# A third residual buffer, a fifth transposed context and new turn tables for a four-layer transformer kernel

## The chip, the cores and the metric

One Trainium2 chip, one of its cores. The metric is the device time of one run of the kernel in microseconds (us); smaller is better. A core has five engines that run side by side, each through its own instruction list: PE (matmul), DVE (vector), ACT (activation functions and copies), POOL (elementwise work) and SP (which here only issues DMAs). They meet through semaphores.

## What is computed

The reference runs eight batches of 256 rows by 256 columns through four layers of attention and feed-forward work, each with a residual addition. Cut to its frame:

```python
x = x + L0_xattn(layernorm(x), ctx)              # 16 heads of 16, softmax
x = x + L0_ffn(layernorm(x), gate_w, expert_w)   # one expert of eight for each row
x = x + L1_xattn(layernorm(x), ctx)              # 16 heads, with a fixed mask
x = x + L1_ffn(layernorm(x), ...)                # three cycles: small nets give a factor, x += factor * twist(x)
x = x + L2_xattn(layernorm(x), ctx)              # linear attention
x = x + L2_ffn(layernorm(x), ...)                # linear layer and two of eight low-rank experts
x = x + L3_xattn(layernorm(x), ctx, mask)        # one head
x = x + L3_ffn(layernorm(x), ...)                # silu(x wg) * (x wu), then wd
```

Every batch goes through all four layers by itself; batches share only the weights.

## The kernel before

The kernel is written straight for the five engines. Each engine's program is a set of threads (Python generators) that emit instructions: `p` prepares an attention (norm, projections, splitting the projections into bf16 parts), `s` is the scores with their softmax, `v` the products with the values, the output projection and the experts of layer 0, `a` the net of layer 1's feed-forward part and linear attention, `b` the rest of layers 2 and 3 for batches 0 to 6, and `c` the same for batch 7. On PE there are two more, `w` and `z`, early and late fillers: every step of theirs issues two matmuls of a constant bf16 tile `blank` into a bank that nobody reads (`spin`, L2002 to L2004). They compute nothing.

What order the instructions of an engine stand in is decided by one string for each engine in `TURNS`: `weave` (L169) reads it letter by letter and lets the named thread go one step. An engine then works strictly through that list, and an instruction whose semaphore is not there yet holds up all that stands behind it. Moving a letter therefore changes no work, only who waits behind whom. Threads `w` and `z` run only as often as their letters occur: 106 and 54 times, which with the 16 filler matmuls ahead of all threads makes 336.

The attentions of layers 0 and 1 run in the order (batch 0, layer 0), (1, 0), (0, 1), (2, 0), (1, 1), and so on, so that two or three batches are under way at any time. The parts of this machine that the change and the prediction touch:

- The scores of a head are computed twice. `L1629` gives them for the row maximum, which DVE reduces (`L1177`). The maximum goes back into the operands by a small transpose (`L1695`) and a copy by ACT (`L873`). `L1714` then gives the transposed scores, ACT takes their exponential into `PT` (`L886`), and `L1736` multiplies with the values. The transposed scores have one PSUM bank, so that the next pair of `L1714` waits for ACT's `L886` on the pair before.
- `L1657` is the product with the eight experts of layer 0 (32 wide matmuls for a batch), which DVE adds up by `L1230`.
- `L1318` on DVE is the step x + factor * twist(x) of layer 1's net: two pairs of quarter tiles, cc with one sign and cn with the other.
- `L634`, `L635` and `L637` on POOL split the keys of an attention into bf16 parts (`kparts`). POOL also computes the scale of every norm (`L615` to `L630`).
- `XB` holds the residual rows of a batch from the end of layer 1's attention until they are stored. There are two, and the first write for batch b waits on DVE until the store of batch b - 2 has landed (semaphore `stored`, L1293 and L1294).
- `ctxT` holds transposed contexts, `CTX` of them: three buffers and the place of the weight wq3t, which is free again by the time a fourth context comes.

## Time and profile before

| what | value |
|---|---|
| median of three runs | 987.79 us (986.56 to 989.19) |
| span of the profiled execution | 986.1 us |
| PE busy | 949.3 us (96%) |
| of that in filler matmuls (`blank`) | 44.7 us, 336 of them |
| DVE, ACT, POOL busy | 634.1, 536.3, 221.5 us |

Busy time is the time in which an engine has an instruction under way, and the matmuls of PE overlap each other a little. The fillers count as busy, so PE's share says less than it seems at the two ends of the program, where most fillers are. The program has three stages for this purpose: a start, in which weights arrive and the first batches fill the machine, a long middle from about 228 to 892 us without any filler, and an end in which batch 7 runs alone.

### The profile page before, as it was taken

The numbers are of one execution on the slowest core, as the hardware profiler recorded it, in microseconds if no ns is written. First come the engines' busy times: TensorE is split into PE (matmuls) and PEld (weight loads), VectorE is DVE, ScalarE is ACT, GpSimd is POOL, SyncE is SP. The second block draws the span as 40 slices with busy tenths as digits, with TensorE's granted clock in tenths as the row PEclk, the third lists the DMA queues.
The fourth block names the chain that finished last, engine by engine and source line by source line (L and its number), as shares of the span: only waits on it lengthen the run. The fifth ranks groups of instructions, "written<-read, shape, count | busy, mean of one in ns | idle before, by whom it ended". The sixth has DMA issues, their size and how long they took to land.

```text
span 986.1 us, 17493 instructions
## 1 busy us (share of the span) xinstructions
PE 949.3 (96%) x6126; PEld 702.7 (71%) x6126; DVE 634.1 (64%) x2245; ACT 536.3 (54%) x1097; POOL 221.5 (22%) x317
## 2 busy tenths in 40 slices
PE   8999999989999999999999999999999999999998
PEld 6665665757687766778687766776686757777777
DVE  4634674675675776867586776775776676736564
ACT  1341644776368643875448644866376544864421
POOL 3104311303240132403141023302321032012210
PEclk9999999999999999999999999999999999999999
DMA  7308535400540023520432104402132004000000
GB/s 261 58 30 226 127 113 113 88 10 17 113 94 9 11 50 70 113 49 13 80 73 46 44 1 86 98 11 49 27 67 59 12 17 92 1 12 1 1 1 22
DMA packets 41078, 58.27 MB, mean 59 GB/s; under 512 B 4096, under 2 KB 35840, under 8 KB 37376
## 3 DMA queue, kind: packets, MB, share of 16 engines
q1 hardware_dynamic: 39600, 48.59, 23.6%
q10 hardware_dynamic: 1392, 8.56, 2.3%
q8 instruction: 50, 0.82, 0.3%
q14 instruction: 36, 0.29, 0.1%
HBM read 41.67 MB, written 13.89 MB: 56 GB/s over the span
## 4 chain that ended last, share of the span: by engine, by line
PE 77%; ACT 9%; DVE 8%; issue 4%; POOL 1%; DMA 1%; ACTq 0%; SPq 0%; DVEq 0%; POOLq 0%
PE bank L1657 11%; PE bank L1984 6%; PE bank L1517 6%; PE bank L1736 6%; PE bank L1714 6%; PE bank L1508 6%; PE bank L1629 4%; PE bank L1995 4%; PE bank L1771 4%; PE bank L1765 3%; PE bank L1717 3%; ACT PT L886 2%; ACT QA L873 2%; PE bank L1797 2%; PE bank L1526 2%
## 5 line engine op out<-in xcount | busy, mean ns | idle before, releaser
L886 ACT ACTIVATE PT<-bank 128x512 f32<-128x512 f32 x256 | 153.0, 598 | 127.4 <-PE bank L1717 71.8
L1657 PE MATMUL bank<-w,xhT 128*128 128x512 f32 x256 | 126.8, 599 | 0.0
L1714 PE MATMUL bank<-QA,KA 104*128 104x256 bf16 x512 | 112.7, 273 | 12.4 <-ACT PT L886 10.5
L1184 DVE CUSTOM_DVE_ANT_0 bank<-bank,maskb 128x256 f32<-128x256 f32 x256 | 101.7, 450 | 25.7 <-PE bank L1629 25.4
L1177 DVE TENSOR_REDUCE mx<-bank 128x2 f32<-128x512 f32 x128 | 83.6, 684 | 28.9 <-PE bank L1629 28.5
L1629 PE MATMUL bank<-KA,QA 96*128 96x256 bf16 x512 | 91.1, 273 | 1.9 <-DVE mx L1184 0.8
L1984 PE MATMUL bank<-xhBT,wi 128*128 128x256 f32 x336 | 87.0, 390 | 2.9 <-DVE hT L1491 2.5
L1714 PEld LDWEIGHTS bank<-QA,KA 104*128 104x128 bf16 x512 | 46.5, 99 | 60.3 <-issue 45.8
L1230 DVE SCALAR_TENSOR_TENSOR x<-bank,one,x 128x256 f32<-128x256 f32 x128 | 61.5, 481 | 21.6 <-PE bank L1657 17.6
L873 ACT COPY QA<-bank 8x256 bf16<-8x256 bf16 (+1 forms) x128 | 67.8, 575 | 10.1 <-PE bank L1695 8.8
L1984 PEld LDWEIGHTS bank<-xhBT,wi 128*128 128x128 f32 x336 | 59.2, 191 | 12.9 <-DVE hT L1491 5.6
L1629 PEld LDWEIGHTS bank<-KA,QA 96*128 96x128 bf16 x512 | 47.5, 100 | 25.3 <-DVE mx L1184 3.2
L1717 PE MATMUL bank<-maskb,identb 128*128 128x256 bf16 x256 | 63.5, 273 | 0.0
L1736 PE MATMUL bank<-PT,vaug 128*32 128x256 f32 x1024 | 63.2, 388 | 0.0
L615 POOL TENSOR_TENSOR veps_s<-mv_s,epsm 128x2 f32<-128x2 f32 x16 | 3.1, 194 | 255.3 <-DVE mv_s L1067 255.3
L1657 PEld LDWEIGHTS bank<-w,xhT 128*128 128x128 f32 x256 | 42.0, 190 | 20.8 <-issue 17.1
L1771 PE MATMUL bank<-xhAT,w 128*128 128x256 f32 (+1 forms) x216 | 49.5, 361 | 0.3
L629 POOL TENSOR_TENSOR veps_a<-mv_a,epsm 128x2 f32<-128x2 f32 (+1 forms) x18 | 3.6, 198 | 204.7 <-DVE mv_a L1067 202.3
L1736 PEld LDWEIGHTS bank<-PT,vaug 128*32 128x32 f32 x1024 | 30.4, 111 | 25.9 <-issue 9.9
L2004 PE MATMUL bank<-blank 128*128 128x256 bf16 x336 | 44.7, 279 | 1.1 <-POOL blank L743 1.1
L1279 DVE RECIPROCAL rc<-bank 128x8 f32<-128x8 f32 x64 | 13.0, 203 | 49.1 <-PE bank L1749 48.4
L1995 PE MATMUL bank<-wi,hT 128*128 128x256 f32 x168 | 42.2, 382 | 0.1
(311 smaller groups left out, 2028.3 us busy)
## 6 DMA issues: line engine op xcount, KB each, us to landing
QA<-scratch SPq DMA_DIRECT2D x90, 128.0 KB, 4.8
scratch<-kparts SPq DMA_DIRECT2D x30, 192.0 KB, 2.4
KA<-scratch SPq DMA_DIRECT2D x15, 384.0 KB, 4.6
scratch<-qparts SPq DMA_DIRECT2D x30, 192.0 KB, 2.3
KA<-scratch SPq DMA_DIRECT2D x15, 256.0 KB, 5.5
w<-pack ACTq DMA_DIRECT2D x1, 2345.0 KB, 8.3
wi<-ipack ACTq DMA_DIRECT2D x1, 2304.0 KB, 8.5
xin<-x_in SPq DMA_DIRECT2D x8, 256.0 KB, 6.3
```

Source lines behind the costliest of these rows:

```text
L873: act.copy(QA[m][KR:KM, g * GH + lo:g * GH + hi, :], ot_b16[KR:KM, 512:512 + S].unsqueeze(1).to_broadcast([MR, hi - lo, S])).then_inc(negm ...
L886: act.activation(PT[:, n % RING, :, :].rearrange("p t s -> p (t s)"), st_bank[:, :], ACT.Exp).then_inc(exp_s, 1)
L1177: dve.tensor_reduce(mx[:, i % 4, n % GH, :], s_bank[n % 2][:, :].rearrange("p (t s) -> p t s", t=T), AX.X, ALU.max).then_inc(max_s, 1)
L1184: last = dve.tensor_tensor_reduce(s, s, maskb[:, t, :], op0=ALU.add, op1=ALU.max, scale=1.0, scalar=-HUGE, accum_out=mx[:, i % 4, n % GH, ...
L1629: last = pe.matmul(s_bank[n % 2][:, t * S:(t + 1) * S], QA[m][0:KR, u, t * P:(t + 1) * P], KA[m][0:KR, u, :], start=True, stop=True)
L1657: last = pe.matmul(bank[n % 2][:, :], xhT[:, kk, t * P:(t + 1) * P], W("exp0", KT)[:, kk, i * 512:(i + 1) * 512], start=(kk == 0), stop=(k ...
L1714: last = pe.matmul(st_bank[:, t * S:(t + 1) * S], KA[m][0:KM, v, t * P:(t + 1) * P], QA[m][0:KM, v, :], start=True, stop=(m == 0))
L1717: last = pe.matmul(st_bank[:, t * S:(t + 1) * S], identb[:, :], maskb[:, t, :], start=False, stop=True)
L1736: last = pe.matmul(pv_bank[32 * h:32 * h + 32, g % 2 * S:(g % 2 + 1) * S], vflat[m][:, t, (g * GH + h) * VW:(g * GH + h) * VW + 32], PT[:, ...
L1771: last = pe.matmul(ps[:, k * S + lo * P:k * S + hi * P], W(name, KT)[:, kk, k * P:(k + 1) * P], src[:, kk, lo * P:hi * P], start=(kk == 0) ...
L1984: last = pe.matmul(ps[:, i * S + lo * P:i * S + hi * P], ww[:, kk, k * P:(k + 1) * P], L.xhBT[:, kk, lo * P:hi * P], start=(kk == 0), stop ...
L1995: last = pe.matmul(ps[:, t * D:(t + 1) * D], hid[:, kk, t * P:(t + 1) * P], wd[:, kk, :], start=(kk == 0), stop=(kk == HT - 1))
```

## The change

`XB` gets a third buffer and `ctxT` a fifth, and every string in `TURNS` is replaced. In the core of the diff the lines that only replace `b % 2` by `b % NX` are left out, and of the strings the beginning of one stands for all:

```diff
-CTX = 4
+CTX = 5
+NX = 3
...
     "tensor":
-        "pppwwwppwwwwwwwwwwwwwwwwppwwwwwwwwwwwwpwwwwwpwpwwwwwwppwwwwwwwwwwwwwwwwwwwsswwspspssvsvswwvsvpsvswwv"
+        "wpppwpwwwwwpwwpwwwpwwpwwwwpwwwpwwwpwwwwpwwwwswswwswpswspvsvwswsvswwspvwvwwwsswvvspvvswsvpwwwvwswvvwv"
...
-        XB = [sb(f"XB{i}", [P, T, D]) for i in range(2)]
+        XB = [sb(f"XB{i}", [P, T, D]) for i in range(NX)]
...
-                        if b >= 2:
-                            dve.wait_ge(stored, nth(stored, b - 2, 16))
-                        update(XB[b % 2], ot_bank, xb1, added)
+                        if b >= NX:
+                            dve.wait_ge(stored, nth(stored, b - NX, 16))
+                        update(XB[b % NX], ot_bank, xb1, added)
```

Each thread has as many letters as before, but for PE's fillers: `w` goes from 106 to 77 and `z` from 54 to 33, so that 236 filler matmuls are left of 336. By `CTX` the tile that the last batch takes for its gate (`sg`, `p3T`) is now `ctxT[3]`, before `ctxT[0]`. The line numbers after the change are one higher from L40 on.

What the strings do is seen in the instruction lists. PE in the first part of the start: `L1508` and `L1517` are projections of batch 0. `L1517` here gives the values, which DVE adds a bias to and writes into `vaug` (semaphore `v_s0`), and `L1535`, the first step of preparing linear attention, waits for that. Before:

```order
L1508 MATMUL bank<-xh0T,w 128x256 x3
L2004 MATMUL bank<-blank 128x256 x32
L1517 MATMUL bank<-w,ctxT 128x256 [waits k_f0,w_in2]
L1517 MATMUL bank<-w,ctxT 128x256 x3
L2004 MATMUL bank<-blank 128x256 x24
L1535 MATMUL bank<-w,ctxT 128x16 [waits q_f0,v_s0]
```

and now:

```order
L1518 MATMUL bank<-w,ctxT 128x256 [waits k_f0,w_in2]
L1518 MATMUL bank<-w,ctxT 128x256
L2005 MATMUL bank<-blank 128x256 x6
L1518 MATMUL bank<-w,ctxT 128x256 x2
L2005 MATMUL bank<-blank 128x256 x4
L1536 MATMUL bank<-w,ctxT 128x16 [waits q_f0,v_s0]
```

The 24 fillers ahead of the wait for `v_s0` have become four.

PE just ahead of the first scores of the program, which wait for `q_first` and `k_first` (the first queries and keys have landed); `L1560` is the last step of preparing linear attention's operands (`sx`). Before:

```order
L1556 MATMUL bank<-w,xh0T 128x16 [waits third_dve]
L1560 MATMUL bank<-w,sx 128x256 [waits third_dve]
L1560 MATMUL bank<-w,sx 128x256
L2004 MATMUL bank<-blank 128x256 x38
L1629 MATMUL bank<-KA,QA 128x256 [waits q_first,k_first]
```

and now:

```order
L1557 MATMUL bank<-w,xh0T 128x16 [waits third_dve]
L2005 MATMUL bank<-blank 128x256 x8
L1561 MATMUL bank<-w,sx 128x256 [waits third_dve]
L1561 MATMUL bank<-w,sx 128x256
L2005 MATMUL bank<-blank 128x256 x8
L1630 MATMUL bank<-KA,QA 128x256 [waits q_first,k_first]
```

The 38 fillers that stood last before the first scores have become eight, and eight more stand one step ahead.

DVE in batch 5's net, at about 738 us: the four steps of `L1318`, among maxima of scores (`mx`, `mq`) and the last multiplications of the gate (`sg`, `hT`) that PE waits for. Before:

```order
L1177 TENSOR_REDUCE mx<-bank 128x2 [waits s_ps]
L1196 TENSOR_SCALAR mq<-mx 128x2x4 [waits mT_ps,max_s]
L1197 SCALAR_TENSOR_TENSOR mq<-mx,mq 128x2x4 [waits dve_s]
L1318 SCALAR_TENSOR_TENSOR o<-xhA,cc 128x2x64
L1318 SCALAR_TENSOR_TENSOR o<-xhA,cn 128x128
L1318 SCALAR_TENSOR_TENSOR o<-xhA,cc 128x2x64
L1318 SCALAR_TENSOR_TENSOR o<-xhA,cn 128x128
L1489 SCALAR_TENSOR_TENSOR sg<-sg,bank 128x256 [waits sg_s]
L1491 TENSOR_TENSOR hT<-sg,bank 128x256 [waits dve_b]
```

and now:

```order
L1490 SCALAR_TENSOR_TENSOR sg<-sg,bank 128x256 [waits sg_s]
L1492 TENSOR_TENSOR hT<-sg,bank 128x256 [waits dve_b]
L1178 TENSOR_REDUCE mx<-bank 128x2 [waits s_ps] x2
L1319 SCALAR_TENSOR_TENSOR o<-xhA,cc 128x2x64
L1319 SCALAR_TENSOR_TENSOR o<-xhA,cn 128x128
L1178 TENSOR_REDUCE mx<-bank 128x2 [waits s_ps]
L1197 TENSOR_SCALAR mq<-mx 128x2x4 [waits mT_ps,max_s]
L1198 SCALAR_TENSOR_TENSOR mq<-mx,mq 128x2x4 [waits dve_s]
L1490 SCALAR_TENSOR_TENSOR sg<-sg,bank 128x256 [waits sg_s]
L1492 TENSOR_TENSOR hT<-sg,bank 128x256 [waits dve_b]
```

One gate multiplication now stands ahead of the net's step, and the step is in two pairs: the second comes after two more gate multiplications.

## Rows read from the trace of the kernel before

**Rows 1.** The page: the span, and busy time of each engine

```profile
span 986.1 us, 17493 instructions
...
PE 949.3 (96%) x6126; PEld 702.7 (71%) x6126; DVE 634.1 (64%) x2245; ACT 536.3 (54%) x1097; POOL 221.5 (22%) x317
```

**Rows 2.** Stretches: length, busy of PE, PEld, DVE, ACT, POOL; granted clock, DMA share, GB/s

```profile
0.00:70.00 70.00, 61.29 (x451) 45.84 (x452) 30.91 (x82) 24.57 (x52) 12.33 (x25) 1.00 0.41 113
70.00:228.00 158.00, 147.13 (x937) 97.84 (x936) 99.25 (x349) 85.16 (x176) 38.59 (x46) 0.98 0.46 110
228.00:730.00 502.00, 497.32 (x3194) 370.36 (x3193) 346.04 (x1219) 297.10 (x591) 130.79 (x178) 1.00 0.26 53
730.00:750.00 20.00, 17.98 (x123) 12.95 (x122) 16.56 (x35) 12.83 (x26) 4.71 (x5) 0.91 0.53 117
...
892.00:986.10 94.10, 86.60 (x546) 71.92 (x543) 52.40 (x211) 30.59 (x96) 14.51 (x32) 0.98 0.02 6
```

**Rows 3.** Stretches of the tile blank alone: length, busy of PE, PEld, ACT, POOL

```profile
0.00:70.00 70.00, 24.77 (x186) 18.75 (x186) 0.20 (x1) 0.31 (x1) 1.00 0.41 113
...
892.00:986.10 94.10, 13.90 (x108) 10.48 (x107) 0.00 (x0) 0.00 (x0) 0.98 0.02 6
```

**Rows 4.** Tile XB: a store (start, duration); its first writes (duration, first and last start)

```profile
879.74 0.39 SPq L589 DMA_DIRECT2D out<-XB  x1
...
L1253 DVE TENSOR_TENSOR XB<-bank,xb x8: 657/690/692, 174.7 to 892.3; 128x512 f32<-128x512 f32 x8
```

**Rows 5.** PE's timeline in the start: start, duration, instruction [idle before, releaser]

```profile
18.79 2.78 PE L2004 MATMUL bank<-blank 128*128 128x256 bf16 x24
22.48 1.06 PE L1535 MATMUL bank<-w,ctxT 128*128 128x16 f32 x8 [0.91 <-DVE vaug L1089]
```

**Rows 6.** Ahead of the first scores: chain of waits; SP's timeline; page on DMA issues

```profile
31.33 4.15 PE bank L2004 x38
...
25.93 3.25 SPq L528 DMA_DIRECT2D QA<-QA  x3
...
QA<-scratch SPq DMA_DIRECT2D x90, 128.0 KB, 4.8
```

**Rows 7.** 93 to 100 us: stretch, timelines of PE, DVE, POOL; undisturbed L1080 (ns)

```profile
96.00:98.00 2.00, 2.00 (x7) 1.53 (x6) 0.00 (x0) 0.64 (x5) 1.14 (x1) 0.50 0.94 114
...
94.95 0.66 PE L1526 MATMUL bank<-w,xh 128*128 128x128 f32 x4 [1.32 <-DVE xh L1080]
...
99.72 1.03 PE L1517 MATMUL bank<-w,ctxT 128*128 128x256 f32 x4
...
93.32 1.57 DVE L1080 TENSOR_SCALAR xh<-x,mv_s,rstd_s 128x256 f32<-128x256 f32 x2 [1.09 <-POOL rstd_s L616]
...
93.46 1.28 POOL L634 TENSOR_TENSOR kparts<-kf,kparts 128x512 bf16<-128x512 f32 x1 [0.17 <-ACT kf L777]
```

**Rows 8.** Around 738 us: a stretch, timelines, and L1318 (ns min/median/max) over the run

```profile
744.00:746.00 2.00, 2.00 (x9) 1.34 (x8) 1.88 (x4) 0.28 (x1) 0.00 (x0) 0.51 0.98 240
...
743.38 1.46 PE L1984 MATMUL bank<-xhBT,wi 128*128 128x256 f32 x4 [2.01 <-DVE hT L1491]
...
739.96 1.20 POOL L635 TENSOR_TENSOR kf<-kf,kparts 128x512 f32<-128x512 f32 x1
...
L1318 DVE SCALAR_TENSOR_TENSOR o<-xhA,cn x32: 342/346/1304, 192.5 to 924.0; 128x128 f32<-128x128 f32 x32
```

**Rows 9.** Waits of PE: us in total, times, longest; page: ACT's exponential, mean ns

```profile
PE bank L1714 <- ACT PT L886: 10.5, 34, 1.0
...
L886 ACT ACTIVATE PT<-bank 128x512 f32<-128x512 f32 x256 | 153.0, 598 | 127.4 <-PE bank L1717 71.8
```

**Rows 10.** The end: PE's timeline where batch 7 begins alone, and a stretch

```profile
892.06 2.13 PE L2004 MATMUL bank<-blank 128*128 128x256 bf16 x18
...
904.00:906.00 2.00, 1.92 (x8) 1.68 (x8) 0.85 (x4) 0.87 (x4) 0.00 (x0) 0.62 0.00 0
```

More of the change, by code:

```diff
@@ new lines @@
+        "ppppppppppvvppvvvvpvvvvvpvvvvvvvvvvvpvpssspppbsssbpvvbpvvvvpvbvvvvpvvvvvvvbvvbvbvbpvbpvvvvvsvvbvvbvv"
+        "vvvvvvvvvvbvvpbpsbpasaavavavvvbvavpvvvpvaapvvvvvpvavavvvvbabvpapavbabvasvvvvvbbvvvavavpvvvvvbvbvvvvb"
+        "vspbpsabbaavabavbvppavvbvabvvvvvbpavbvvvvabavvvvavvpavaaabvvvvvavavpvvvpvsvbvvbvvvvvvbvvbbvpbspapsab"
+        "avavabvvpvbpvavvbvvavbapvbvvvbvavavavpvvavaaavbpvpavvavvsvpvvvbvbvvvpbpvvvvvvbvvvbbvssbababvabppavbv"
+        "vavpbvvavvvvbavaavvavvvbvpavvvvavaapavvvpvvvavasvvvvbbvvvvvbvvvbvvbpvbvsppbsababvaavavvbvpvavpvvvbvp"
@@ new lines @@
+        "avbvvvvvabavavavvvavabpavavsvvvvvavvavvvvvvvvvbvbvvvbvpbpabbsasabpabavvbvvvpvpbvvvvvbvvvvbvavvvavbva"
+        "vaavvvavvvbvasapaavvpvvavavvvvvbvvbvsvsvbvvcbabbaavavbavvvbavvbvabvavbavabvvvavvbvavaavavvbvaavbabaa"
+        "aaaaabaaaaaaaaaaaabaaaaaaaaaabbaaaabbcccbcbcbcbcbccccccccccccccccccc",
+    "vector":
+        "pppvppvpppvppppssspsspsssssssssssssssvvpvpvpvspsspssssssssssppsssssssspsssbssssssssssssvssssvssspsvs"
+        "vpsspssvsssssssspssvpsvssvvsssvasasssssssspsssaaasbssspspsssssssssssvsssssssavssaapsvvssppsvssppaaaa"
+        "asassaabsbsvsbbbbbbsbvvsvssbbsbvaabspsspsbbssbspsaaabsssbssssbssssbsssssbsssvbssavsaassbsvvssvaaaaaa"
+        "sbssspssappbabsbsbbsvbbbssbbpsbbbvssbvspvssvsababbssssspssspsspbasaasbssssbsssbsbssbvsssaaasssssvsss"
+        "sbssvpaavaaapsvpasssbspsapabbsbbbbbsbbbsbsbvsbssbvvsvssbsbvabpapssssbsssbssbsspsbssasabasssssbsssssb"
+        "sasvaassssvssspvvspsbvsaaapabassasspsapabsbssbbbbbbbvsssbbbbsvsvsvsbsbvabaspsbssssbpssssssaaasbsssps"
+        "ssssbsssbssssvssbssssaassasbsvvvsvssasaaapasbasbsaabvbsbsbbbbbbvsvvpbbpbvasasbssspbpbbssssssbsssassb"
+        "ssassbsspssbasvbvsssssbssssvsvsssvaasasbsssssssbbsaasaasasasasabssbsvsbsvbbbbbbpvvbbbvacabssssbsbssb"
+        "sssaaasbsbsssbsbsssbsaaabvbaaavaaavbvabcabvabaaabbbbbbbaaaabbbaaaabaaaaaaaaaabbaabacacccbcccccbccccc"
@@ new lines @@
+        "svsvpbvvsvvsvssvpvvssvvpvssvsvvsvspvsvssvvsspsvvpvwvvsvsvsvvssvsvspvvvvsvsvvsvsvpvsvssvvsvsvsvswvvwp"
+        "psassaasspssassvavspassvvvspvsasvpavvvsvasspvsavsspsvsvpsvsvsasvpvsvspssavssvvvasvpsvavavvpavpavsapp"
+        "vvsvsvsvsvvsavsvavsavsvsvvbsvsvvsvbsvsvsvvsbvsvbvbpvpsvbssbpbaspsabsasbbsspavpasbavbbsvabsvsbvsavabs"
+        "vbssasvbvsvpbvssvvbabvsvspvssvbbpsavbbsbvvbsvsbvabvsvavasbvbvavavapvsvbspvbvvasbsvavpvavvpvpsvvbvsvb"
+        "ssvsvsvvssvsvsvbsbpbvvssbsbbvsssbvsvpvvpbbpsassaassbpspsasbvasvsasbpvpvsvsbbasvspbsvbvavvassbbvssavv"
@@ L135 @@
+        "assbsbasvpsvsbbssvvpsvsbvbsvpvbvpvsvssbvvvvbvbavpvvvavasbssvbsassvvsbsavbvsavsbsvvbsvbvpbsavsbsvvsba"
+        "vabvbsabasassssvsvsvssvsasassvsavvsvssvbvvbvvpvsvssvpbvbvbvvcvcvcbcbbacabssasbsbsasvavsasbsvvsbvbavs"
+        "abvbsvabbsvvasbbavsbsbavvvvbabvavvavvbbabbvabbavbbvvbvabavbvavvbabaaaaaaaabaaabbaaaaaaaaaaabazabaaaa"
+        "aabaaaazazzzzzzzzzzzbzzbbzaaaaaazbzbbccccbbzzzzzzbbzzzzzzcbbcccbbzzzcbbcccbcbcccbbbcbccccccccccccccc"
+        "cccccccccccccccc",
 }
@@ L575, in last @@
                     sp.wait_ge(final.s["xb_new"], at(final, "xb_new", b, 3, h))
-                    sp.dma_start(out[b, lo * P:hi * P].rearrange("(t p) d -> p t d", p=P), XB[b % 2][:, lo:hi, :]
+                    sp.dma_start(out[b, lo * P:hi * P].rearrange("(t p) d -> p t d", p=P), XB[b % NX][:, lo:hi, :]
                                  ).then_inc(stored, 16)
@@ L588, in rest @@
                     sp.wait_ge(xb_new, nth(xb_new, b, 3))
-                    sp.dma_start(out[b].rearrange("(t p) d -> p t d", p=P), XB[b % 2][:, :, :]).then_inc(stored, 16)
+                    sp.dma_start(out[b].rearrange("(t p) d -> p t d", p=P), XB[b % NX][:, :, :]).then_inc(stored, 16)
                     yield
@@ L710, in net @@
                     for h, lo, hi in parts(b):
-                        plus(o2, XB[b % 2], "bao", xba_s, lo, hi)
+                        plus(o2, XB[b % NX], "bao", xba_s, lo, hi)
                         yield
@@ L729, in rest @@
                             pool.wait_ge(dn_ps, nth(dn_ps, b - 1, 1))
-                        plus(L.xbB, XB[b % 2], "blin", L.s["xbb_s"], lo, hi)
+                        plus(L.xbB, XB[b % NX], "blin", L.s["xbb_s"], lo, hi)
                         yield
```

53 lines of the change are left out of this document (13 added, 40 removed).

## The prediction

> **What bounds the kernel now.** I read the busy times first, then the same times by stretch, then the waits and timelines in the stretches that lose. PE is busy for 949.3 of 986.1 us, DVE for 634.1 [rows 1], so PE's work or PE's waits set the time. By stretch the waits lie at the two ends. In the first 70 us PE is busy for 61.29 us, of which 24.77 us are fillers [rows 2, 3], so that 33.5 us pass without useful matmuls. From 70 to 228 us it is idle for 10.9 us. From 228 to 730 us it idles 4.7 us of 502 [rows 2], which is what an order can at best give back there. From 730 to 750 us there are 2.0 us of idle time and a granted clock of 0.91 in place of 1.00. After 892 us batch 7 is alone: 94.1 us less 86.6, and of those 13.9 us fillers [rows 2, 3], hence 21.4 us without useful work. The amount of useful work doesn't change, so a gain has to come from the two ends or from a few single places, and a loss can come from anywhere.
>
> **The buffers.** They take away no wait that the trace shows. The tightest case of the residual rows is the last: the store of batch 5 is issued at 879.74 us and batch 7 writes the same buffer first at 892.3 us [rows 4], with 12 us between. Where DVE waits, no store of XB ended the wait, and no arrival of a context ended a wait of PE. Term: 0. What may count is that an order with other overlaps becomes legal, and this is in the next terms.
>
> **The start.** Ahead of the first scores 38 fillers run for 4.15 us, 0.109 us each, and they end at 35.48 us on the chain [rows 6]; if the operands came earlier, the rest of the fillers only held up PE. The last three transfers of QA are issued from 25.93 us on for 3.25 us; each issue takes about a third of that, so the last begins near 28.1 us. With 4.8 us to land, as another transfer of QA has it [rows 6], they are there at about 33 us, at 34 us if the landing counts from the end of the issue. With eight fillers in place of 38, and eight more one step ahead, PE comes to the scores at about 33 us (31.33 plus 0.9 for either group). So the first scores are 1.5 to 2.5 us earlier; I take 1.8 us.
>
> Against this stands the clock. The new order has eight fillers fewer ahead of the end of L1517 (24 for 32), so L1517 ends at 18.79 - 0.87 = 17.9 us, and of the 24 fillers that followed four are left, inside that count. Then PE waits for `v_s0`, which comes at about 22.5 us (DVE has the same work ahead of it). It was 0.91 us idle there [rows 5] and will be 4.6 us. The trace shows what shorter waits do: after 1.32 us of idle time at 94.95 us the granted clock of the stretch from 96 to 98 us is 0.50, that is the 1.2 GHz level [rows 7], and after 2.01 us at 743.38 us it is 0.51 [rows 8]. One such fall costs, by the clock of 0.91 from 730 to 750 us, 9% of 20 us = 1.8 us [rows 2]. In the start some of that lies in hops in which PE waits for DVE anyway; I take 1.0 us. Term: -1.8 + 1.0 = -0.8 us, between -2.5 (no fall) and +1.8 us (two falls of 1.8 us less the 1.8 us gained).
>
> The Trainium skill has a rule that speaks against this part: by "TensorE: Matmul & The Clock Gate", section "HAM oscillation — how this bites in real kernels", a wait of PE for data between two bursts of matmuls lets the clock fall to its half, and the next burst begins slow. The two falls above agree with it; by that page the start would bring no gain, which is the mechanism of the third case below.
>
> From the first scores to the end of that attention PE waits on the round trip of one bank at a time, and the new order keeps the same pairs in the same sequence; its fillers there are 62 for 46, 16 of 0.109 us = 1.7 us more, in places where PE idled or spun anyway. No term.
>
> **93 to 100 us.** PE waits 1.32 us for the normalised rows of batch 0 (xh). DVE took 1.57 us for two tiles that cost 0.41 us each elsewhere, while POOL's L634 ran from 93.46 us [rows 7]. In the new order this POOL step waits until xh is written, which takes 0.75 us off, and PE has two matmuls of the next projection ahead of its wait. I expect the idle time of 1.32 us to go. In exchange `L1560` has moved out of a wait into the run of the experts, where PE is full: four matmuls of that size take 1.0 us [rows 7]. If PE stays dense, the fall of the clock at 96 us goes too, 1.8 us as above. That makes -1.32 + 1.0 - 1.8 = -2.1 us, or -0.3 us with the fall. I take -1.5, bounds -2.1 and +1.0.
>
> **738 us.** Four steps of L1318 stood in a row on DVE; three of them took up to 1.30 us in place of 0.346 while POOL split keys (L635 1.20 us at 739.96 us), and PE waited 2.01 us behind them for hT [rows 8]. With the fall of the clock this place costs 2.0 + 1.8 = 3.8 us. Now one gate multiplication goes ahead, and the four are two pairs with gate multiplications between, so that a collision with POOL delays hT by two steps of 0.96 us at most and finds PE with one more block of work. I take -2.5 us; -3.8 if all of it goes, 0 if the first pair collides and the clock falls again.
>
> **What the new order may lose in the middle.** The transposed scores are the tightest loop. PE lost 10.5 us in 34 waits for ACT there; the exponential alone takes 0.598 us [rows 9], and with the hand-overs a pair can start about 0.96 us after the pair before is through. I added up PE's work between each two pairs in both orders, with the durations of before: it is under 0.96 us in 51 places before, by 11.7 us in all, and in 61 places now, by 17.2 us. In proportion the 10.5 us become 15.4, a loss of 4.9 us. Over half of the difference lies in the first 200 us, where other waits and fillers cover it. I take +1.5 us, bounds 0 and +4.9.
>
> **The end.** The late fillers go from 108 to 66 matmuls: 42 of 0.109 us, 4.6 us, but they stood in waits, as the 2.13 us at 892.06 us [rows 10], and PE will be idle there in their place. A fall of the clock is there already (0.62 from 904 to 906 us [rows 10]); it may come some us earlier or once more. Term 0, bounds -0.7 (six fillers that PE ran while their operand was ready) and +1.8 us.
>
> **The sum.** -0.8 - 1.5 - 2.5 + 1.5 + 0 = -3.3 us. The profiled execution has a span of 986.1 us, 1.7 us under the median of 987.79; I carry that difference over: 986.1 - 3.3 + 1.7 = 984.5 us. What a measurement of this kernel can tell from no change is about 0.3%, 3 us, and the forecast lies just beyond that.
>
> **The rivals.**
> 1. No difference, about 987.5 us. The middle has no slack to give, the buffers remove no wait (the change then doesn't do what the buffers promise), and collisions of POOL with DVE only move to another batch. Then 738 us brings -1.0, the start -0.8, 93 us -0.3, and the transposed scores cost two fifths of the way to their bound, +1.9: -0.2 us. For it speaks that PE's landmarks (the ends of each batch's parts) stand at the same amount of PE work in both orders; against it, that the two stalls at 95 and 743 us have a visible cause which the new lists take apart.
> 2. Slower, about 992.5 us, by the clock where fillers were. The wait of 4.6 us in the start and the wait at 892 us without its 18 fillers each end at the 1.2 GHz level, and thin matmuls with hops between keep it there. Start +1.8, end +1.8, 738 us 0 (a fall there too), the middle +1.5, 93 us -0.3: +4.8 us. It decides once the start has two falls in place of one, since from there on its gain is gone. For it speak the falls after waits of 1.32 and 2.01 us [rows 7, 8]; against it, that at 22 us much of PE's slow work would lie in hops that wait for DVE.
>
> **How the numbers follow.** Forecast (faster by over 0.3%, below 984.8 us): 0.48, with a range of its own from 978 to 984.8. No difference: 0.31. Slower by over 0.3%, above 990.8 us: 0.21, in which a new stall that I don't see in the lists has its part. The lower bounds of all terms add up to -9.1 us, the upper ones to +9.5 us, that is 978.7 and 997.3 us; that all fall to the upper side at once is unlikely, and 978 to 995 us leaves out about one in ten at either side.
>
> **What would show it.** First scores before 34.3 us and a granted clock near 1.0 from 22 to 26 us: the start as forecast or better; first scores at 35.5 us or later: the second rival. An idle time of PE under 0.4 us ahead of the transposes of xh at about 93 us, and a clock of 1.00 there. At about 738 us no wait of PE for hT over 0.5 us and no L1318 over 1 us. PE's waits for ACT's exponential at 12 us in all; at 15 us or more the middle has lost what the rest gained. The forecast is wrong from the ground up if PE has a single new wait of over 3 us between 228 and 892 us, or if a store of XB ends a wait.

## The result and the profile after

The changed kernel takes 1007.79 us (median, 1005.87 to 1010.25) against 987.63 us of the kernel before beside it: a ratio of 1.021, interval 1.0187 to 1.0233. That is slower by 20 us, where 984.5 us was forecast. The page of the profile after: span, busy times and one group (busy, mean ns | idle time ahead of it):

```profile
span 1006.5 us, 17296 instructions
...
PE 951.7 (95%) x6026; PEld 700.0 (70%) x6026; DVE 627.0 (62%) x2245; ACT 536.6 (53%) x1097; POOL 220.9 (22%) x317
...
L1715 PE MATMUL bank<-QA,KA 104*128 104x256 bf16 x512 | 113.2, 274 | 21.4 <-ACT PT L887 15.5
```

PE's busy time rose by 2.4 us although 100 fillers fewer run, and the span by 20.4 us [rows 1]. To find the place, I took from PE's timelines the end of the output projection of each of the 16 attentions (q0 to q15) in both traces and subtracted:

| stretch | before, us | after, us | difference | what it is |
|---|---|---|---|---|
| start to the end of q0 | 70.0 | 75.3 | +5.3 | two falls of the clock to the 1.2 GHz level, and 2.0 us at full clock |
| q0 to q1 | 67.5 | 75.9 | +8.4 | a load beside a store, 7.2 of it |
| q1 to q3 | 91.1 | 91.9 | +0.8 | |
| q3 to q12 | 479.4 | 487.9 | +8.5 | many starts a little late |
| q12 to q13 (738 us before) | 62.5 | 59.3 | -3.2 | the stall is gone |
| q13 to the end | 215.6 | 216.2 | +0.6 | |

A stretch is only as good as its repeats. From q3 to q12 the old order takes 479.4 to 479.5 us in six traces (before, experiments 1, 5, 8, 11 and the third kernel of 6), and the new one 487.9 to 488.0 us in four (the changed kernel and those of 2 and 4), so the 8.5 us there are not chance. The start is less steady: with the old order q0 ends between 69.6 and 74.1 us.

The stretches of after that answer to [rows 2] (length, PE busy and matmuls, granted clock, DMA share, GB/s):

```profile
18.00:24.00 6.00, 1.48 (x9) 0.70 0.57 102
24.00:36.00 12.00, 11.89 (x56) 0.58 0.75 119
...
114.00:124.00 10.00, 7.39 (x31) 0.66 0.97 183
...
730.00:750.00 20.00, 20.00 (x111) 1.00 0.00 1
```

**Start.** PE's timeline after (start, duration, instruction [idle ahead, who ended it]):

```profile
22.93 1.89 PE L1536 MATMUL bank<-w,ctxT 128*128 128x16 f32 x8 [4.52 <-DVE vaug L1090]
...
36.99 0.38 PE L1630 MATMUL bank<-KA,QA 96*128 96x256 bf16 x2
```

The wait of 0.91 us of [rows 5] has become 4.52 us. Behind it the clock stays near half for some 12 us, and the first scores start at 36.99 us, not at 35.3. From there to the end of q0 another 3.6 us are lost. About half of them lie in the output projection itself, which meets a second fall of the clock (0.72 from 70 to 76 us); here before, then after:

```profile
68.05 1.98 PE L1517 MATMUL bank<-w,attT 128*128 128x256 f32 x8
```

```profile
71.60 3.66 PE L1518 MATMUL bank<-w,attT 128*128 128x256 f32 x8
```

**q0 to q1.** Timelines after, of PE, POOL, SP's queue, ACT's queue and ACT, of the keys of the second attention:

```profile
102.07 1.16 POOL L635 TENSOR_TENSOR kparts<-kf,kparts 128x512 bf16<-128x512 f32 x1 [0.85 <-DVE xh L1081]
...
105.60 0.90 SPq L462 DMA_DIRECT2D scratch<-kparts  x2
...
105.84 0.33 ACTq L856 DMA_DIRECT2D wi<-ipack  x1
...
114.93 0.47 ACT L776 ACTIVATE kparts<-bank,w 128x256 bf16<-128x256 f32 x1 [5.59 <-DMA scratch<-kparts]
...
116.20 0.61 PE L1715 MATMUL bank<-QA,KA 104*128 104x256 bf16 x2 [2.95 <-ACT QA L874]
```

and the two transfers in the kernel before, on SP's and ACT's queues:

```profile
97.17 0.90 SPq L461 DMA_DIRECT2D scratch<-kparts  x2
...
126.68 0.34 ACTq L855 DMA_DIRECT2D wi<-ipack  x1
```

Before, 29 us lay between the store of the split keys and the load of `wi`, 2304 KB. After, the store leaves 8.4 us later and ACT issues the load 20.8 us earlier: they meet within 0.24 us. Of the 8.4 us, 5.3 are the late start, which moves both transfers; counted from the end of q0, the new order puts the store 3.2 us later and the load 26 us earlier. The split's wait for xh makes up at most 1 us of that (in experiment 7, where POOL's order alone is new, the store leaves at 98.13 us). ACT's next keys may overwrite `kparts` once the store has landed, and wait 5.59 us for it, until 114.9 us, 9 us after the issue. Behind them in ACT's queue stands the copy of QA (L874), and PE waits 2.95 us for that; the clock falls to 0.66. No wait of ACT for a DMA stands in the trace of before.

**738 us.** The stretch is full at a clock of 1.00, and the net's steps no longer collide with POOL. Tile o after (ns min/median/max):

```profile
L1319 DVE SCALAR_TENSOR_TENSOR o<-xhA,cn x32: 342/345/348, 207.3 to 944.8; 128x128 f32<-128x128 f32 x32
```

**The middle, q3 to q12.** The stretch before and after (length, PE busy, clock), then PE's groups in it before and after (busy, mean ns | idle ahead and who ended it):

```profile
228.60:708.00 479.40, 474.72 (x3074) 1.00 0.26 53
...
243.10:731.00 487.90, 478.57 (x3075) 1.00 0.25 52
```

```profile
L1714 PE MATMUL bank<-QA,KA 104*128 104x256 bf16 x288 | 64.1, 272 | 2.7 <-ACT PT L886 2.0 <-ACT QA L873 0.2
L1984 PE MATMUL bank<-xhBT,wi 128*128 128x256 f32 x192 | 49.0, 385 | 0.1
L1629 PE MATMUL bank<-KA,QA 96*128 96x256 bf16 x256 | 46.5, 272 | 0.3 <-DVE mx L1184 0.3
...
L1822 PE MATMUL bank<-w,xhAT 128*128 128x1 f32 x52 | 6.8, 234 | 0.2 <-ACT xhAT L944 0.2
```

```profile
L1715 PE MATMUL bank<-QA,KA 104*128 104x256 bf16 x288 | 64.1, 272 | 4.7 <-ACT PT L887 3.2 <-ACT QA L874 0.7
L1985 PE MATMUL bank<-xhBT,wi 128*128 128x256 f32 x192 | 48.8, 384 | 0.8 <-DVE hT L1492 0.7
L1630 PE MATMUL bank<-KA,QA 96*128 96x256 bf16 x256 | 46.6, 272 | 0.8 <-DVE mx L1178 0.7
...
L1823 PE MATMUL bank<-w,xhAT 128*128 128x1 f32 x52 | 6.8, 234 | 1.0 <-ACT g L948 1.0
```

The counts, the durations and the clock are the same; the busy times of all groups add up to 616.8 us before and 617.3 after. What changed is how densely they follow each other. The idle time grew from 4.7 to 9.3 us, and the other 3.9 us lie inside PE's busy time, where pipelined matmuls overlap less when a start is a little late (their ends are modelled, so this half is a reading). An estimate from the starts in the two timelines: each block's distance to the next, less the lower quartile for its kind, gives delays of over 0.1 us that add up to 15.2 us before and 20.9 us after: +2.1 at the transposed scores, +1.1 at the scores, +1.0 at L1823 (which waits for ACT), +0.7 at the transposes of xh, +0.6 at L1985, and the rest evens out. The sums shift by about a microsecond with the way blocks are grouped, and they place 5.7 of the 8.5 us; the other 2.8 lie in smaller steps that this doesn't place. The longest wait of PE there is 0.87 us.

### The profile page after: what moved, and what is told of

Its sections match the earlier page's. It is cut to its first block, busy times and chain, and to the rows that moved or that the text cites. A ratio compares the mean times of both kernels' runs of the same rounds, so it can differ in the third digit from the quotient of the medians.

```text
span 1006.5 us, 17296 instructions
## 1 busy us (share of the span) xinstructions
PE 951.7 (95%) x6026; PEld 700.0 (70%) x6026; DVE 627.0 (62%) x2245; ACT 536.6 (53%) x1097; POOL 220.9 (22%) x317
## 4 chain that ended last, share of the span: by engine, by line
PE 76%; ACT 9%; DVE 9%; issue 3%; DMA 1%; POOL 1%; ACTq 0%; SPq 0%; DVEq 0%; POOLq 0%
PE bank L1658 11%; PE bank L1985 7%; PE bank L1737 6%; PE bank L1518 6%; PE bank L1715 6%; PE bank L1509 5%; PE bank L1772 4%; PE bank L1630 4%; PE bank L1996 4%; PE bank L1766 3%; PE bank L1718 2%; ACT PT L887 2%; PE bank L1798 2%; PE bank L1527 2%; ACT QA L874 2%
## 5 line engine op out<-in xcount | busy, mean ns | idle before, releaser
L1715 PE MATMUL bank<-QA,KA 104*128 104x256 bf16 x512 | 113.2, 274 | 21.4 <-ACT PT L887 15.5
L1630 PE MATMUL bank<-KA,QA 96*128 96x256 bf16 x512 | 94.5, 277 | 2.4 <-DVE mx L1178 1.2
L1985 PE MATMUL bank<-xhBT,wi 128*128 128x256 f32 x336 | 85.2, 384 | 2.0 <-DVE hT L1492 1.5
L874 ACT COPY QA<-bank 8x256 bf16<-8x256 bf16 (+1 forms) x128 | 67.8, 575 | 20.0 <-PE bank L1696 18.6
L1985 PEld LDWEIGHTS bank<-xhBT,wi 128*128 128x128 f32 x336 | 58.8, 189 | 11.9 <-DVE hT L1492 3.9
L1518 PE MATMUL bank<-w,ctxT 128*128 128x256 f32 x168 | 45.4, 395 | 0.4
L1509 PE MATMUL bank<-ctxT,w 128*128 128x256 f32 x168 | 43.9, 389 | 0.2 <-ACT w L983 0.2
```

Of the source, the lines that this page charges most:

```text
L874: act.copy(QA[m][KR:KM, g * GH + lo:g * GH + hi, :], ot_b16[KR:KM, 512:512 + S].unsqueeze(1).to_broadcast([MR, hi - lo, S])).then_inc(negm ...
L1509: last = pe.matmul(ps[:, k * S:(k + 1) * S], W(name, KT)[:, kk, k * P:(k + 1) * P], src[:, kk, :], start=(kk == 0), stop=(kk == KT - 1))
L1518: last = pe.matmul(ps[:, t * D:(t + 1) * D], src[:, kk, t * P:(t + 1) * P], W(name, KT)[:, kk, :], start=(kk == 0), stop=(kk == KT - 1))
L1630: last = pe.matmul(s_bank[n % 2][:, t * S:(t + 1) * S], QA[m][0:KR, u, t * P:(t + 1) * P], KA[m][0:KR, u, :], start=True, stop=True)
L1715: last = pe.matmul(st_bank[:, t * S:(t + 1) * S], KA[m][0:KM, v, t * P:(t + 1) * P], QA[m][0:KM, v, :], start=True, stop=(m == 0))
L1985: last = pe.matmul(ps[:, i * S + lo * P:i * S + hi * P], ww[:, kk, k * P:(k + 1) * P], L.xhBT[:, kk, lo * P:hi * P], start=(kk == 0), stop ...
```

## The experiments

**1. The buffers alone.** The kernel before with both sizes, and the old order.

```diff
-CTX = 4
+CTX = 5
+NX = 3
```

> The kernel before with the buffers of the change alone: three residual buffers and five transposed contexts, all turn strings as before. Theory: no wait of the trace ends with the store of a residual buffer or with a context, so the time is that of the kernel before, 987 us, within 1.5 us. Rival: the buffers let DVE or PE run ahead at the end of the batches and give 2 us or more; or they cost something by their place in memory.

987.85 us, ratio 1.0007 (0.9993 to 1.0021). The buffers by themselves do nothing that can be measured; all else is the order.

**2. The load out of the store's way.** The changed kernel with the load of `wi` issued in the first batch.

```diff
                             load(6)
+                            act.dma_start(wi[:, :].bitcast(I32), ipack).then_inc(wi_in, 16)
                             yield
...
                     elif b == 1:
-                        act.dma_start(wi[:, :].bitcast(I32), ipack).then_inc(wi_in, 16)
                         yield
```

> The changed kernel with one DMA moved: ACT issues the load of the last layer's integer weights (wi, 2304 KB) right behind the last piece of w, at about 80 us, and no longer at 105.84 us. Theory: in the changed kernel this load, issued 0.24 us after the store of the split keys (scratch<-kparts at 105.60 us), holds that store up until 114.9 us; ACT waits 5.6 us for it, PE waits 2.95 us at 116 us, and the granted clock falls to half from 116 to 123 us. Without it the store lands within 3 us, the wait of PE and the fall go, and the time comes down by 6 to 7 us, to about 1001 us. Rival: the store is late because POOL splits these keys later than before; then the wait stays and the gain is under 1 us.

1000.50 us (1.0136, 1.0101 to 1.0172), 7.3 us under the changed kernel. From q0 to q1 it takes 68.7 us in place of 75.9, and ACT no longer waits for the store. So 7.2 us of the loss hang on where this one load is issued.

**3. The same from the other side.** The changed kernel with POOL's order of before, so that the split no longer waits for xh.

```diff
     "gpsimd":
-        "pppppppppppsspsssppspsppssssppppsasppssapspppsssapaabbppbsbasspbspsbpppapaaabpsbsbppsbbbsabppssbaspp"
+        "ppppppppssppsppsppsssppspssppsppssappsspsssasppaapapbbppbsbpsabssppbapbsaappsapbsbbspbpssabbbppssppp"
...
```

> The changed kernel with GpSimd's order of before, the other four engines as changed. If GpSimd's new order (the split normalization factors that wait for their rows) causes the loss in the middle, the stretch from the fourth to the thirteenth attention falls from 488 us to 484 or less. If the orders of VectorE and ScalarE cause it, it stays at 487 or more. GpSimd's old order was placed against the old VectorE order, so a new wait of 1 to 3 us at one place is possible either way. At the start, the store of the partial sums should leave at about 98 us, ahead of the 2.3 MB load issued at 106, and the wait of 5.6 us on ScalarE for it should be gone: the whole then 7 us under the changed kernel, 1000 us.

Its SP and ACT queues, and ACT's keys:

```profile
100.73 0.90 SPq L462 DMA_DIRECT2D scratch<-kparts  x2
...
101.95 0.33 ACTq L856 DMA_DIRECT2D wi<-ipack  x1
...
109.72 0.47 ACT L776 ACTIVATE kparts<-bank,w 128x256 bf16<-128x256 f32 x1 [2.55 <-PE bank L1509]
```

(The expectation's "partial sums" are the split keys.) The load is still early, but the store leaves 1.2 us ahead of it, and the wait on ACT is gone: q0 to q1 in 70.5 us. The two stores still took 6.7 us in the median to land, against 5.6 us in the changed kernel; what has changed is that ACT has its keys to write 9.0 us after the issue, and not after 3.7 us. The whole, one run, was 1011.38 us, not 1000: the middle lost 6 us more (494.1 us; one wait of PE for xhA is 2.91 us) and the end 3 us, as it may where the old POOL order stands beside a new DVE order. So POOL's new order had its part in the wait at 105 us. Whether it costs in the middle this run doesn't show, because the mixture brings waits of its own.

**4. PE kept busy in the start.** 38 fillers put ahead of the wait for `vaug` in the changed kernel; then these, 36 more in eight later waits, and the early load together.

```diff
     "tensor":
-        "wpppwpwwwwwpwwpwwwpwwpwwwwpwwwpwwwpwwwwpwwwwswswwswpswspvsvwswsvswwspvwvwwwsswvvspvvswsvpwwwvwswvvwv"
+        "wpppwpwwwwwpwwpwwwpwwwwwwwwwwwwwwwwwwwwwpwwwwpwwwpwwwpwwwwpwwwwswswwswpswspvsvwswsvswwspvwvwwwsswvvs"
...
```

> The changed kernel with 38 more filler matmuls in the one wait of 4.5 us at 18.4 us (for the values of batch 0). Nothing else is moved. Theory: the half clock from 20 to 34 us comes from this wait; with it filled the granted clock stays at 1.0, the first scores come at about 33.5 us in place of 36.99, and the time falls by 3 to 3.5 us, to about 1004.5 us. Rival: the first scores wait for the transfer of the queries, and what is gained is given back before the end of the first attention: under 1 us.

> The changed kernel with the load of wi moved ahead, the 38 fillers in the wait at 18.4 us, and 36 more fillers in eight waits of 0.3 to 0.8 us between 48 and 147 us. Theory: besides the two effects (6.5 and 3 us) the three falls of the granted clock at 71, 81 and 147 us go, 1.8 us each, so that about 15 us come back and the time is about 992 us; the rest against the kernel before are new waits in the middle (about 9 us from 189 to 731 us, less 3.2 us gained at 738 us). Rival: fillers in short waits cost what they fill, the falls stay, and the sum is that of the two other runs, about 997 us.

With the 38 alone 1005.16 us (1.019, 1.0158 to 1.0221): 2.6 us less in the median, though the interval overlaps that of the changed kernel. Only 0.38 us of the wait is left, yet the clock falls to 0.50 from 28 to 32 us (mean 0.79 from 20 to 36), and the first scores come at 36.10 us, not at 33.5. So the wait of 4.5 us alone isn't what lowers the clock there. With everything 997.92 us (1.0113, 1.0082 to 1.0144), where 15 us of gain were expected and 9.9 came, the sum of the two other runs, as the rival had it. In that run the clock is 1.00 from 20 to 175 us, q0 ends at 72.0 us, and PE waits ahead of the first scores for something else. Here, and then the same place in the kernel of 10 that keeps the old order:

```profile
35.38 0.38 PE L1630 MATMUL bank<-KA,QA 96*128 96x256 bf16 x2 [3.47 <-DMA QA<-QA]
```

```profile
34.50 0.60 PE L1630 MATMUL bank<-KA,QA 96*128 96x256 bf16 x4 [1.37 <-DMA QA<-QA]
```

The last three transfers of QA are issued from 27.11 us on in the first of these runs and from 25.89 us in the second: the operands are there 8.3 and 8.6 us after that. In the kernel before, which issues them from 25.93 us on, that puts them at an estimated 34.2 to 34.5 us, about 1 us ahead of the first scores at 35.32. That was all there was to win. Of the 5.3 us of the start the clock is 3.3 (75.3 against 72.0 us). The other 2.0 stay at full clock, 1.9 of them behind the first scores; what makes them is open. The rest of the loss of this version is above all the middle (488.0 us).

**5. The old start with few fillers.** The kernel before with 24 fillers cut to 4 and 38 to 8.

```diff
-        "pppwwwppwwwwwwwwwwwwwwwwppwwwwwwwwwwwwpwwwwwpwpwwwwwwppwwwwwwwwwwwwwwwwwwwsswwspspssvsvswwvsvpsvswwv"
+        "pppwwwppwwwwwwwwwwwwwwwwppwwpwwwwwpwpwwwwwwppwwwwsswwspspssvsvswwvsvpsvswwvssvpvvssvpsvwwwvvvvwwvpvv"
...
```

> The kernel before with fewer fillers in the start alone: 4 in place of 24 ahead of the wait for the values of batch 0, and 8 in place of 38 ahead of the first scores. Theory (the clock): PE idles for about 4.4 us, the granted clock falls to half from 20 us on as in the changed kernel, and the first scores come at about 37 us in place of 35.48, so the time rises by 1 to 2 us, to about 989 us. Rival (the fillers only held up PE): the clock stays at 1.0, the first scores come at 33 to 34 us, and the time falls by 1.5 to 2.5 us.

987.41 us (1.0008, 0.9991 to 1.0026). PE waits 3.10 us for `vaug`, the clock falls (0.79 from 20 to 36 us), the first scores come 0.7 us earlier, and q0 ends at 70.1 us, as before. The theory of this run, 1 to 2 us more by the clock, failed, and its rival, 1.5 to 2.5 us less, too. So removing these fillers is not enough for the loss: it needs the rest of the new start too.

**6. The old order up to a point, the new one from there.** All five lists are cut at the end of q3, q8 or q12 (228, 500, 708 us), and the buffers are those of the changed kernel; of the first cut POOL's line in which the lists part:

```diff
     "gpsimd":
-        "ppppppppssppsppsppsssppspssppsppssappsspsssasppaapapbbppbsbpsabssppbapbsaappsapbsbbspbpssabbbppssppp"
+        "ppppppppssppsppsppsssppspssppsppssappsspsssaspppapaabbppbsbasspbspsbpppapaaabpsbsbppsbbbsabppssbaspp"
...
```

> Buffers of the change. On every engine the order of before up to the end of the fourth attention (about 228 us), from there on the order of the change. Theory: what the changed kernel loses after 229 us is a loss of its order there and not a late effect of its start: +8.4 us to 708 us, -3.2 us at 738 us, +0.7 us to the end, so about 993 us. Rival: the losses in the middle are inherited from the late start (buffers and queues out of step), and with the old start the time is at 987 us or, with the gain at 738 us, at 984 us.

> Buffers of the change. The order of before up to the end of the ninth attention (about 500 us), from there on the order of the change. Theory (losses lie where the landmarks show them): +4.2 us from 500 to 708 us, -3.2 us at 738 us, +0.7 us to the end, so about 988.5 us. Rival (inherited): 984 us.

> Buffers of the change. The order of before up to the end of the thirteenth attention (about 708 us), from there on the order of the change, which has the two pairs of the net's step at 738 us and fewer fillers in the end. Theory: the stall of 2.0 us and the fall of the clock at 743 us go and bring 3.2 us, the end costs 0.7 us, so that the time is about 984.5 us, below the kernel before. Rival: the gain at 738 us is taken back by the end of the program, 987 us.

996.26, 990.67 and 987.91 us (1.0086, 1.0035, 1.0008; intervals 1.007 to 1.0102, 1.0022 to 1.0047, 0.9996 to 1.0021). The loss grows with the length of new order in the middle. The medians differ by 5.6 us between the first and the second kernel and by 2.8 us between the second and the third; in the traces the new order costs 4.7 us from q3 to q8 (first kernel) and 4.2 to 5.7 us from q8 to q12 (first and second). From q3 to q12 the first takes 488.3 us, as the changed kernel does (488.0), behind a start that wasn't changed. The loss is therefore made in place and isn't the late shadow of the start. All three came out 2 to 3.5 us above what was expected. The last one was to gain 3 us by the stall at 738 us. It ran q12 to q13 in 61.0 us, and its profiled start had a fall of the clock that the same PE order doesn't have in the profile of before; in the other two it fell as well (q0 ends at 73.6 to 74.1 us in the three). Stretches of the last (PE busy, clock), then of before:

```profile
26.00:28.00 2.00, 2.00 (x12) 0.62 0.86 113
28.00:30.00 2.00, 2.00 (x7) 0.50 1.03 90
```

```profile
26.00:28.00 2.00, 1.88 (x11) 1.00 0.81 98
28.00:30.00 2.00, 1.83 (x15) 1.00 1.08 99
```

What the fall cost there shows in PE's timeline ahead of its first scores at 39.35 us:

```profile
35.20 4.31 PE L2005 MATMUL bank<-blank 128*128 128x256 bf16 x38
```

The fall made PE late, the operands had by the estimate of experiment 4 been there since about 34.5 us, and the 38 fillers still ran in full. In experiment 5 the clock fell too, but with eight fillers there the first scores came at 34.58 us. By this reading the 30 fillers cost about 1 us at most where the clock stays up, and some 3 us (30 of 0.109 us) where it falls.

**7. POOL's new order alone** (with the buffers) in the kernel before.

```diff
     "gpsimd":
-        "ppppppppssppsppsppsssppspssppsppssappsspsssasppaapapbbppbsbpsabssppbapbsaappsapbsbbspbpssabbbppssppp"
+        "pppppppppppsspsssppspsppssssppppsasppssapspppsssapaabbppbsbasspbspsbpppapaaabpsbsbppsbbbsabppssbaspp"
...
```

> The kernel before with the buffers and with POOL's order of the change; all other engines in the order of before, so that the load of wi stays at 126.68 us. Theory: POOL's order is harmless by itself and helps at 93 us: DVE writes xh without POOL beside it, PE's wait of 1.32 us falls to about 0.6 us, and the split keys are stored some us later without anyone waiting, since no large load is under way then. Time 984.5 to 987 us. Rival: POOL's order is what costs in the changed kernel (the later split delays the store of the keys, and ACT behind it), and the time rises by 3 us or more.

991.55 us (1.0038, 1.0021 to 1.0055), 3.6 us slower, as the rival had it but not for its reason: no wait of ACT for the store. The wait at 94.95 us fell from 1.32 to 0.48, as the prediction had it, but at 503 us POOL now splits keys ahead of a normalisation that PE is waiting for. DVE's and PE's timelines:

```profile
502.84 0.73 DVE L1081 TENSOR_SCALAR xh<-x,mv_s,rstd_s 128x256 f32<-128x256 f32 x2 [4.16 <-POOL rstd_s L617]
...
503.63 0.66 PE L1527 MATMUL bank<-w,xh 128*128 128x128 f32 x4 [3.21 <-DVE xh L1081]
```

**8. The stall at 738 us alone.** The kernel before with eight of DVE's turns rearranged: hT ahead, the four steps of L1318 in two pairs.

```diff
-        "asssaabsspsbssvbvsssssbsssvsvsassvassabssssssssbsaasaaasasbssasabbsssvbsbbbvbbbvpvbbbvacabssssbsbssb"
+        "asssbssapsbassvbvsssssbsssvsvsassvassabssssssssbsaasaaasasbssasabbsssvbsbbbvbbbvpvbbbvacabssssbsbssb"
```

> The kernel before with two letters of DVE's string moved: at 738 us the gate multiplication that PE waits for goes ahead of the four steps of L1318, which become two pairs. Theory: PE's wait of 2.0 us for hT and the fall of the granted clock behind it go, -3.2 us as the landmarks of the changed kernel have it, so about 984 us. Rival: the steps collide with POOL all the same and hold up the maxima of scores behind them, so that half or less of it is left.

984.45 us (0.9974, 0.9959 to 0.999). From q12 to q13 it takes 58.9 us in place of 62.5. The stretch of [rows 8] there:

```profile
730.00:750.00 20.00, 19.61 (x142) 1.00 0.52 111
```

This is the gain that the prediction had, and here it comes without the rest of the change.

**9. What the middle hangs on: the exponential?** ACT's exponential over half of the columns from the ninth head on (the other half isn't computed), in the kernel before with the buffers and in the first kernel of 6.

```diff
-                                           st_bank[:, :], ACT.Exp).then_inc(exp_s, 1)
+                            c = T * S if n < RING else S
...
+                                           st_bank[:, 0:c], ACT.Exp).then_inc(exp_s, 1)
```

> The kernel before with the buffers; ACT takes the exponential of one half of the columns only (from the ninth head on), so that L886 takes about 0.38 us in place of 0.60. Half of the softmax is left out. It is the base for the next run: from the end of the fourth attention to that of the thirteenth it should take at most 2.5 us less than the 479.4 us of the kernel before, since its waits for the exponential there are 2.0 us in all.

> The same half exponential in the kernel that has the order of before up to the fourth attention and that of the change from there on. With whole exponentials it takes 488.3 us from the fourth to the thirteenth attention, 8.9 us more than the kernel before. Theory (the loop of scores, exponential and one bank is what the new order has too little work in): with 0.2 us off each round trip the difference to the run with the old order falls from 8.9 to 4 us or less. Rival (waits for DVE, or queues standing in each other's way): the difference stays at 7 us or more.

972.18 us (0.9846, 0.9815 to 0.9877) and 981.67 us (0.9946, 0.9924 to 0.9968). The stretch q3 to q12, old order, then new:

```profile
223.60:696.80 473.20, 471.04 (x3072) 1.00 0.26 54
```

```profile
222.80:706.40 483.60, 475.39 (x3076) 1.00 0.27 55
```

L886 takes 0.39 us in the mean in place of 0.60, and PE's waits for it in the stretch go from 2.0 us to none in the old order and from 3.3 to 0.7 us in the new. Both orders gain, 6.2 and 4.7 us, and the distance is 10.4 us, no smaller than 8.9. If the exponential's round trip made the loss, it would have shrunk to 4 or less. That theory falls. The old order was expected to gain 2.5 us at most, hardly more than its waits; it gained 6.2, more than the 4.7 us that PE is idle there at all. So the exponential delays PE by more than the visible waits, in the old order too, and idle time isn't the limit of what this stretch can give back.

**10. DVE's maxima?** The same pair with DVE's maxima of the scores over half the columns (the other half is left out).

```diff
-                        dve.tensor_reduce(mx[:, i % 4, n % GH, :], s_bank[n % 2][:, :].rearrange("p (t s) -> p t s", t=T),
+                        dve.tensor_reduce(mx[:, i % 4, n % GH, :], s_bank[n % 2][:, :].rearrange("p (t s) -> p t s", t=T)[:, :, 0:P],
...
-                            s = s_bank[n % 2][:, t * S:(t + 1) * S]
+                            s = s_bank[n % 2][:, t * S:t * S + P]
```

> The kernel before, three buffers and five transposed contexts, with VectorE's maxima of the scores taken over half the columns (the other half is left out, so each maximum is shorter on VectorE). The stretch from the fourth attention's output projection to the thirteenth's takes 479.4 us in the kernel before and 488 us with the new order. If VectorE's queue sets what TensorE waits for there, this stretch falls in the old order by 4 us or more; if not, by less than 2 us.

> The old order up to 228 us, the new one from there, with the maxima on VectorE over half the columns (the other half is left out). Theory that the new order's loss in the middle is late results of VectorE's queue (maxima, hT, xhA, xh): the stretch from the fourth to the thirteenth attention falls from 488.3 us to 484 or less, and its difference to the old order with the same cut shrinks from 9 to 5 us or less. Rival, that the loss is many single places on VectorE and ScalarE alike, each set by its own turn and not by how long VectorE is busy: 486 or more, and a difference of 7 us or more stays.

One run each, 980.32 and 995.07 us. The stretch q3 to q12, old order, then new:

```profile
226.70:705.50 478.80, 474.18 (x3072) 1.00 0.25 53
```

```profile
229.10:716.80 487.70, 477.79 (x3076) 1.00 0.26 54
```

0.6 us each, and the distance stays 8.9 us. Neither how long DVE is busy with the maxima nor how long ACT is busy with the exponential sets it. That leaves the rival that was named ahead: single turns of DVE and ACT that stand a little late in their lists for the PE block that needs them, 78 late blocks with 20.9 us as against 73 with 15.2. It fits, but no run shows it. A second rival stands untested beside it, PE's own list: if the lower quartile is taken for each pair of neighbouring kinds (over the traces of both orders) and not for each kind, it adds up to 462.8 us before and 464.9 after, so by this estimate up to 2 of the 8.5 us may lie in which blocks stand side by side on PE. POOL's list isn't cleared either (experiment 3). Which list costs most is open; the orders of DVE, ACT and PE were not exchanged one without the others.

**11. A version that beats both.** The kernel of 8 with 32 fillers in place of 24 ahead of the wait at 22.48 us [rows 5].

```diff
-        "pppwwwppwwwwwwwwwwwwwwwwppwwwwwwwwwwwwpwwwwwpwpwwwwwwppwwwwwwwwwwwwwwwwwwwsswwspspssvsvswwvsvpsvswwv"
+        "pppwwwppwwwwwwwwwwwwwwwwppwwwwwwwwwwwwwwwwpwwwwwpwpwwwwwwppwwwwwwwwwwwwwwwwwwwsswwspspssvsvswwvsvpsv"
...
```

> The kernel before with the eight moved VectorE turns at 738 us and with 32 instead of 24 matmuls on the blank tile ahead of the first wait for the normalized values at 22 us. The eight close the wait of 0.9 to 1.1 us behind which the clock fell to half in the profiled starts that were slow, so that it falls less often: 983 us in the median against 984.5 without them and 987.6 before, and a spread narrower than 981 to 989. If the fall has another cause, 984.5 again.

983.98 us, 0.9955 (0.9936 to 0.9973). The seven runs lie between 983.42 and 984.86 us, where those of 8 lie between 981.42 and 989.37. The clock in the start:

```profile
26.00:28.00 2.00, 1.88 (x12) 1.00 0.88 90
28.00:30.00 2.00, 1.85 (x15) 1.00 1.11 132
```

The median barely moved; the slow end went, and the fast end with it. That fits a fall behind the wait at 22 us as a cause of the spread, but seven runs against twelve don't prove it, and the length of the wait alone doesn't tell the starts apart: the clock fell behind 0.75, 0.76 and 1.13 us (the kernels of 6) and stayed up behind 0.91 us (before and experiment 1).

## Why the prediction was wrong

**A term was missing: the load of `wi`, +7.2 us.** The prediction weighed POOL's later split only as a gain for DVE. It didn't follow the split to its store on SP's queue, and it didn't look at what else ACT issues there. Counted from the end of q0, the order moves the store 3.2 us later and the load 26 us earlier; the second shift stood in ACT's list, and the trace of before had the size of the load. Experiments 2 and 3 take the wait away from either side.

**Start: -0.8 forecast (bounds -2.5 and +1.8), +5.3 measured.** Three steps failed. First, the gain of 1.8 us: the operands were put at 33 to 34 us from issue and landing times of another transfer. They land some 8.5 us after the three issues begin (experiment 4), in the kernel before at 34.2 to 34.5 us, so about 1 us was there to win; experiment 5 won 0.7 at the first scores and nothing at the end of q0. Second, the falls: one was taken, at 1.0 us, and two came. Their price was about right, 3.3 us for both against 1.8 each by the prediction. Third, "No term" for the way from the first scores to the end of that attention: it took 3.6 us more, 1.7 by the second fall and 1.9 that are there at full clock too. The prediction counted 16 more fillers there, 1.7 us, and put them into idle places; whether they are what costs, no run shows. The second rival named this mechanism with +1.8 us; its sign, "first scores at 35.5 us or later", came true at 36.99. The rule of the Trainium skill that the prediction weighed ("TensorE: Matmul & The Clock Gate", section "HAM oscillation — how this bites in real kernels") spoke against this part, and the trace agrees with it in the changed kernel (0.58 behind the wait of 4.52 us, 0.66 from 114 us on). In experiment 4 the clock fell too with 0.38 us of that wait left, and in experiment 5 it fell and cost nothing: the price of a fall has to be read from the stage it falls in.

**93 to 100 us: -1.5 forecast, right in its place.** The wait of 1.32 us is gone, and so is the fall behind it (1.00 from 96 to 108 us). From the projections ahead of it (L1508, L1509 after) to L1869 and L1870 behind it 7.8 us pass in place of 10.7; of these 2.9 us the 1.0 us of L1560 goes off, which now stands among the experts. The gain didn't carry: even with the load out of the way q0 to q1 takes 68.7 us, 1.2 more than before. And the same later split had its part in a wait that cost 7.2 us a little further on.

**738 us: -2.5 forecast, -3.2 measured** (-3.6 in experiment 8). The collision, its place and its price were read rightly.

**Middle: +1.5 forecast (bounds 0 and +4.9), +8.5 measured, and the mechanism was wrong.** PE's waits for the exponential rose from 10.5 [rows 9] to 15.5 us, almost exactly the upper bound of 15.4, which looks like a hit and isn't one. In the middle they rose from 2.0 to 3.2 us; the other 3.8 us lie outside it, in stretches that the clock and the load stretched anyway. Counting tight pairs in one loop took that loop for the whole. The loss is spread over the producers of many blocks, and half of it doesn't even show as idle time. "It idles 4.7 us of 502 [rows 2], which is what an order can at best give back there" was too tight as well: the half exponential took 6.2 us out of that stretch with the same matmuls (experiment 9). Idle time of PE measured neither what could be won there nor what could be lost. Which lists make the 8.5 us stays open; shown is that they are made between q3 and q12 by the new order (experiment 6), and not by how long the exponential or the maxima take.

**Buffers 0 and end 0: right within their bounds, or nearly.** 1.0007 in experiment 1; from q13 on it is +0.6 us against the profile of before, and +1.9 against the old order's other traces (214.3 us in five of them).

**The signs that were to show it wrong from the ground up** (one wait over 3 us between 228 and 892 us, a store of XB) did not occur: the longest single wait there is 0.87 us. A time 23 us off was made without either. The sign should have been a sum over the stretch, not its largest member.

## What to carry to other kernels

When an order moves a step, follow each transfer behind it to its queue and list what other engines issue within 10 us of its new place; a large load there can hold a small store, and behind the store a whole queue. Expect a new order to lose in a stretch in which the bounding engine is 99% busy, as this one did: change the few places with a visible stall by hand (here eight turns gained 3.5 us) and leave the rest. Don't take that engine's idle time for all that can be won or lost there. Before you call a filler removable, find out when the operand behind it lands.

## What the runs showed of the hardware

- A store of split keys lands in 2.3 us in the median (192 KB each). Two of them, issued 0.24 us ahead of a load of 2304 KB on another engine's queue, took 5.6 us in the median and up to 8.8; with the load 1.2 us behind 6.7, and with no such load near 3.3 (experiment 2) and 4.5 (the kernel before).
- With one and the same PE order in the start the clock fell between 26 and 34 us in some runs and not in others, worth up to 4 us at the first scores (39.35 against 35.32 us) where 38 fillers stood behind the fall.
- It also fell where PE had waited only 0.38 us (experiment 4), and stayed up behind 0.91 us.
- In 480 us of dense matmuls 3.9 of the 8.5 us lost show as busy time, with the same matmuls at the same clock (PE busy 474.72 and 478.57 us).
